# Routed experts: tokens before one-hot rows, slot weights after expert 1's transposes, low halves one place sooner

## The reference, cut to what matters

```python
logits = xf @ gate_w.T                      # 576 x 8
top_p, top_i = top_k(softmax(logits), 2)    # two experts a token
w = top_p / top_p.sum(-1, keepdims=True)
pos = cumsum(onehot(top_i))[...] - 1        # place of the choice in its expert
keep = pos < cap                            # cap = 180 slots an expert
buf[expert * cap + pos] = x                 # rows of each expert's slots
z = 2 * buf;  z *= rsqrt(mean(z * z) + 1e-6);  z *= norm_w[expert]
g, u = split(z @ w13[expert].T)             # 192 -> 2 x 512
y = buf + (silu(g) * u) @ w2[expert].T      # 512 -> 192
out = sum over the two choices of w * keep * y[slot]
h = h + out
```

## Time and profile before

| | |
|---|---|
| median of 3 executions | 271.56 us |
| profiled execution, device time | 269.44 us |
| its span, first to last instruction | 267.6 us |
| TensorE matmul busy | 223.1 us (83%) |
| TensorE weight load busy | 174.5 us (65%) |
| VectorE busy | 191.0 us (71%) |
| ScalarE busy | 154.6 us (58%) |
| GpSimd busy | 115.9 us (43%) |
| GpSimd's DMA queue | 13.66 MB, 34.0% of 16 engines' span |
| mean granted TensorE clock | 0.950 |

### The profile page before, as it was taken

How to read it: one execution, slowest core, us unless ns; L and a number is a source line. 1 busy time by engine, 2 the same in 40 slices (tenths; PEclk the granted TensorE clock), 3 DMA queues, 4 the chain that set the end, 5 groups by cost and what they waited for, 6 DMA issues and landing times.

```text
span 267.6 us, 6168 instructions
## 1 busy us (share of the span) xinstructions
PE 223.1 (83%) x2338; PEld 174.5 (65%) x2338; DVE 191.0 (71%) x520; ACT 154.6 (58%) x296; POOL 115.9 (43%) x139
## 2 busy tenths in 40 slices
PE   1964999797396897797989999899899695999992
PEld 1741467586396896344458596786648595899982
DVE  1749979767999577869958869649786352655575
ACT  4639467355679755378579758557461265455610
POOL 9112495011122696476390002502602887867710
PEclk9996599999779599999999999999999999999997
DMA  6999352332540049993009001994290599883362
GB/s 213 336 257 216 82 224 65 71 69 68 164 146 4 2 67 205 212 210 67 4 0 108 2 0 10 119 138 62 13 173 12 100 147 160 144 124 31 35 154 66
DMA packets 24786, 28.66 MB, mean 107 GB/s; under 512 B 11544, under 2 KB 19793, under 8 KB 24533
## 3 DMA queue, kind: packets, MB, share of 16 engines
q0 software_dynamic: 6624, 13.66, 34.0%
q1 hardware_dynamic: 18133, 14.60, 19.2%
HBM read 34.98 MB, written 4.81 MB: 149 GB/s over the span
## 4 chain that ended last, share of the span: by engine, by line
PE 43%; DVE 26%; ACT 9%; issue 8%; POOL 1%; DMA 1%; another core or an unknown queue 1%; DVEq 0%; ACTq 0%; POOLq 0%
PE bank L885 7%; PE bank L896 5%; PE bank L552 5%; PE bank L637 4%; PE bank L568 3%; PE bank L727 2%; PE bank L609 2%; DVE arena_k L1018 2%; PE bank L597 2%; PE bank L704 2%; PE bank L582 2%; DVE st L949 2%; PE bank L834 1%; DMA arena<-x_scratch,arena 1%; PE bank L745 1%
## 5 line engine op out<-in xcount | busy, mean ns | idle before, releaser
L637 PE MATMUL bank<-tri,idh 128*128 128x512 f16 x148 | 38.5, 380 | 0.0
L1797 POOL TENSOR_TENSOR arena<-arena,ri 128x432 f32<-128x432 f32 x8 | 7.5, 942 | 39.3 <-DVE ri L1067 39.3
L1773 POOL TENSOR_TENSOR rs<-arg,mhalf 128x1 f32<-128x1 f32 (+1 forms) x20 | 11.9, 596 | 23.1 <-DVE arg L953 21.6
L1875 POOL DMA_INDIRECT arena<-x_scratch,arena x14 | 14.1, 1006 | 16.7 <-DVE arena L1431 12.7
L1866 POOL DMA_INDIRECT y_sum<-arena x12 | 18.2, 1515 | 6.3 <-issue 2.9
L1383 DVE TENSOR_TENSOR arena<-bank,arena 128x360 f32<-128x360 f32 x16 | 8.4, 532 | 16.8 <-PE bank L885 8.5
L637 PEld LDWEIGHTS bank<-tri,idh 128*128 128x128 f16 x148 | 13.7, 98 | 9.7
L568 PE MATMUL bank<-arena,arena_k 96*128 96x288 f16 (+2 forms) x144 | 18.3, 286 | 0.0
L525 PE MATMUL bank<-arena_v,arena 128*128 128x192 f16 (+1 forms) x90 | 11.6, 295 | 5.9 <-DVE arena_v L967 5.9
L568 PEld LDWEIGHTS bank<-arena,arena_k 96*128 96x128 f16 x144 | 13.8, 98 | 3.5
L885 PE MATMUL bank<-arena,arena_v 128*128 128x180 f16 x160 | 13.4, 240 | 2.9 <-DVE arena L1372 2.6
(11 more groups left out here) (286 smaller groups left out, 634.2 us busy)
## 6 DMA issues: line engine op xcount, KB each, us to landing
arena_k<-in_w POOLq DMA_DIRECT2D x8, 512.0 KB, 6.4
arena_v<-in_w POOLq DMA_DIRECT2D x8, 512.0 KB, 10.2
arena_v<-in_xT SPq DMA_DIRECT2D x6, 288.0 KB, 3.7
arena_v<-in_wqkv SPq DMA_DIRECT2D x3, 576.0 KB, 10.0
arena_v<-v_scratch SPq DMA_DIRECT2D x32, 54.0 KB
v_scratch<-arena SPq DMA_DIRECT2D x4, 384.0 KB, 2.6
arena_k<-in_w POOLq DMA_DIRECT2D x8, 192.0 KB, 7.2
arena_v<-in_w POOLq DMA_DIRECT2D x8, 192.0 KB, 11.2
```

The costliest lines, as they stand in the source:

```text
L637: mm(bank[IDLE][:, :], idh[:, :], tri[:, 0:1].broadcast_to([128, 512]), start=True, stop=True)
L1773: g.tensor_tensor(rs[0:r, o + i:o + i + 1], arg[0:r, o + i:o + i + 1], half_[0:r, 0:1], ALU.pow).then_inc(sem_out, 1)
L1875: nc.gpsimd.indirect_dma_start(zr[:, e - 1, XW * k:XW * k + XW], None, x_scr[:, :], bass.IndirectOffsetOnAxis(ap=tok_at[:, k, e:e + 1], ax ...
```

## The change

TensorE: `tokens_of_slots()` stands ahead of `rows_selected(0)`, `slot_weights()` behind `rows_transposed(1)`, and the numbers of idle matmuls change (8 to 15 after the counts; 1 and 1 become 6 between `rows_selected(0)` and expert 0; 6 become 2 after step 0's transposes). The PSUM banks follow the new order. VectorE: `choices()` stands ahead of `onehots(0)`, and `z_low(0)` behind `token_index()` and `routing_weights()`. GpSimd: low 4 is issued ahead of the layer norm's powers, low 5 where low 4 was, low 6 behind the gathers of expert 2, and high 7 behind those of expert 3. ScalarE: the negation of expert 7 moves from step 1 to step 3.

```diff
         plan("pos")
+        plan("tok")
         plan("z", 0)
-        plan("tok")
...
             fills(ins, "pos")
-            keep_awake(8)
+            keep_awake(15)
...
+            tokens_of_slots()
             rows_selected(0)
-            keep_awake(1)
-            tokens_of_slots()
-            keep_awake(1)
+            keep_awake(6)
             for s in range(E + 1):
                 if s < E:
                     up_gate(s)
-                if s == 0:
-                    slot_weights()
                 if s + 1 < E:
                     rows_transposed(s + 1)
                     if s + 1 in LATE:
                         positions_spread(s + 1)
                 if s == 0:
-                    keep_awake(6)
+                    slot_weights()
+                    keep_awake(2)
...
+            choices()
             onehots(0)
             x_low(range(2, NT))
-            choices()
-            z_low(0)
             token_index()
             routing_weights()
+            z_low(0)
...
-                if s == 1:
+                if s == 3:
                     negate_high(act, 7)
...
             expert_low(pool, 3)
+            expert_low(pool, 4)
...
-            expert_low(pool, 4)
+            expert_low(pool, 5)
...
                 if e == 2:
+                    expert_low(pool, 6)
+                if e == 3:
                     expert_high(pool, E - 1)
-                if 2 <= e < 4:
-                    expert_low(pool, e + 3)
```

## The result

The changed kernel took 274.81 us (median of 4 runs, 274.19 to 276.77), the kernel before on the same chip 271.83 us (4 runs, 271.5 to 273.18). The ratio is 1.0115, 95% interval 1.0066 to 1.0164: slower by 2.98 us, where +2.6 was forecast (274.2 against 271.56).

A forecast was written before the change was run, and what follows sets the result against it. TensorE's chain and GpSimd's adds were taken to arrive together: low 7 3.4 us later less 0.66 gives +2.7, so 272.1 against the profiled 269.44; with the median 2.1 above it, 271.56, forecast 274.2, range 271.2 to 277.0.

The forecast's parts named there:

- Which chain ends last: End of kernel: GpSimd's adds and TensorE's chain arrive together; later adds move the end +2.7 us, giving away TensorE's 2.7.
- Rival A: End of kernel: adds do not bind, TensorE's chain does; faster, 268.5, if expert 2's add is by 239.6; chance 0.12.
- Tokens first: Token matmuls ahead of expert 0: gathers 2.4 us sooner, up_gate(0) 3.06 later, up_gate(1) at 213.4; worth nothing within 0.5.
- Low halves sooner: GpSimd's weight queue: hole ahead of expert 3 goes, up_gate(3) at 224.2 instead of 227.68; worth about 3.5 us to TensorE.
- The negation's end: ScalarE, expert 7's negation in step 3: copy starts at 229.7, takes 3.25 us to negation's end, 232.95; GpSimd waits at low 7.
- The 0.8 us for expert 4's gates: ScalarE's gates of expert 4 and next rows come some 2.5 us late, costing TensorE about 0.8 once.
- Low 7 to the end: GpSimd's queue: low 7 issued 3.4 us later, at 233.25; last add goes from 253.83 to 257.2, last load lands at 264.6.
- the bound: SyncE's last load of the sum: lands at most 3.6 us after its start.
- the slack that was put at 0.66: Before the change, the last load lands at 261.18 and VectorE needs it at 261.84: 0.66 us ahead of need.
- The rule that was weighed: GpSimd DMA takes about 2.0 us plus bytes over 436 GB/s: expert 2's add issue-bound, end about 1.2 us sooner, 273.0.
- Rival C: Whole kernel: little change; low 7 only 2 us late, last add under 1.3; 271.5 to 272.7; chance 0.09.
- Rival B: Late releases of TensorE's results come again; on down(2), negation and adds some 3 us later; slower still, 277; chance 0.13.

## Why the prediction was right

In mechanism it was right: the late negation holds low 7, low 7 holds the adds, the adds hold the end. That the median came within 0.6 us is in part luck. The negation ended 2.15 us later than predicted in the profile (1.2 later from the mark), the profiles differ by 5.1 us where +2.7 was predicted for them, and the interval behind low 7, taken as fixed, is not.

**Which chain ends last.** Held. The adds bind, and TensorE's 1.4 us are given away. Rival A needed expert 2's add at or before 239.6; it is at 245.26. The negation's line by itself decides whether the kernel is slower (0.9987, no change that can be measured, against 1.0115).

**Tokens first: nothing within 0.5.** Held in size. The first gather came at 204.14, so 2.5 sooner once the 0.9 of drift is taken off (2.4 predicted); `up_gate(0)` at 208.49, `up_gate(1)` at 213.92, both within 0.9 of 207.65 and 213.4. Alone it measured 0.9979 with an interval that holds 1. But "worth nothing" holds only for this part alone: beside the low halves it is worth some 3.2 us (0.9987 against 1.0107), which the prediction, adding part to part, has nowhere.

**Low halves sooner: `up_gate(3)` at 224.2.** The wait for rows went, and it started at 225.89, of which 0.5 lies ahead of `up_gate(1)` and 1.16 ahead of `up_gate(2)`. Low 4 did fit ahead of the norm's powers. But its reason was only a part: the hole before was not the queued weights alone. With the old order of the tokens the same move left a hole (1.0107), and 3.5 us were no property of this edit. It depends on which indirect DMAs stand in a row, and perhaps on GpSimd's pause among them.

**The negation's end, 232.95.** It came at 235.10, 2.15 later. 0.52 of that is `up_gate(1)`, 1.16 the late result ahead of `up_gate(2)`, 0.02 the pace, and 0.44 the copy, which started 0.54 after `up_gate(4)`, not 0.10. Of this 0.16 is a slip of reading: 239.21 in the earlier trace rows is where the chain's row of `up_gate(5)` begins; by the timeline TensorE started it at 239.05, so the pattern was 0.26. The drift ahead of the change, 0.9, covers all of `up_gate(1)`'s 0.52. From the copy to the end of the negation it took 235.10 - 231.84 = 3.26, as predicted (3.25). The 0.8 us for expert 4's gates measured 6.12 - 5.41 = 0.7.

**Low 7 to the end.** The interval from low 7 to the last add stayed (23.94), which was luck too: in two other kernels with the same instructions between the two it took 25.71 and 26.13, up to 2.2 us more than the 23.97 that was carried over, and the last load took 3.77 from its issue to the chain's next step, 0.2 above the bound. Last add +5.5, end +5.1 in the profiles; 0.4 was lost to the slack that was put at 0.66. With the 2.15 us above taken off, the last add falls on 257.2, the predicted value.

**The rule that was weighed.** By the sizes of the Trainium skill, DMA: Bandwidth & Descriptors, Anatomy of one DMA, expert 2's add would not wait for a transfer. In the changed kernel it doesn't (idle 0.30, issue), yet the time of the rule, 273.0, is further from 274.81 than the forecast; in the kernel with the negation in step 2 it waits 3.08 us, which the rule does not give. The rows of before were the better guide here, for one reading only: the interval as a whole.

**Rival C.** Low 7 was not 2 us late but 5.5, and the last add as much.

**Rival B.** It happened in a small form in the profiled execution: a late release of 1.2 us and one of 0.4. In the medians, +2.98 against +2.6 predicted, there is room for a fraction of it. How far the 2.1 us by which the first profile lay under its median differ from run to run was not measured by stretches. The prediction said of B that less is queued in that stretch, so it should be rarer; as far as that meant weights the reason was wrong, since late releases come without any in the queue.

## What to carry to other kernels

When two chains end together, ask of each moved step which queue waits on it: here a negation of 2.6 us on an engine with time to spare held up a queue of DMAs in which all later adds stood, and every us of its delay came back at the end. Put a wait in an in-order queue behind the work that doesn't need it. And a gap on TensorE ahead of a transfer's rows is not yet proof that it waits for them: look whether the results behind it come late too, and what kind of DMA is being issued then.

## What the runs showed of the hardware that was not expected

- TensorE slows under a row of GpSimd's indirect DMAs: 20 small matmuls took 5.7 us in place of 1.63, and a reader waited up to 6.66 us for a result, with no releaser in the trace. The recorded ends of matmuls, which are modelled, then seem to run ahead of the true ones (222.7 against a reader's start at 224.58). It was milder in the kernels that have weights or a pause among the gathers. The mechanism stays open, and so does what sets it off.
- After such a hole the granted clock was at the 1.2 GHz level for most of the next stretch (a mean of 0.57 over 230 to 237), and 14 idle matmuls put into the hole kept it at 1.00, for a gain in time within the measurement's error.
- Dependent accumulating adds to one sum followed each other at 4.03 to 4.05 us an expert in the changed kernel, 4.05 to 4.16 before, but 4.05 to 4.36 with the negation in step 2 and 4.14 to 4.57 with the negation alone moved.
